# First attention of a macaron kernel: scores computed once and held in SBUF, the causal mask written by GpSimd

## What is computed

```python
scores = jnp.einsum('bqhd,bkhd->bhqk', qf, kf) * scale
mask = jnp.tril(jnp.ones((s, s), dtype=bool))
scores = jnp.where(mask[None, None], scores, jnp.finfo(scores.dtype).min)
p = jax.nn.softmax(scores, axis=-1)
o = jnp.einsum('bhqk,bkhd->bqhd', p, v).reshape(b, s, H * DV)
return o @ w_out
```

## Time and profile before

| what | value |
|---|---|
| median of 3 runs | 2211.37 us (2203.29 to 2222.01) |
| profiled execution | 2215.39 us |
| its span | 2213.7 us, 33049 instructions |
| PE busy | 1940.7 us (88%) |
| DVE busy | 1626.8 us (73%) |
| POOL busy | 991.4 us (45%) |
| ACT busy | 921.0 us (42%) |
| largest group | L1190 POOL, x528, 585.0 us |
| next | L1224 DVE x640, 385.6 us; L1231 DVE x640, 380.3 us; L1113 ACT x640, 358.0 us |

### The profile page before, as it was taken

One profiled execution on the slowest core, in us unless ns is written; L12 is line 12 of the kernel. 1 busy time (PEld: TensorE's weight loads), 2 busy tenths in 40 slices (PEclk: granted clock), 3 DMA queues, 4 the chain that ended last, 5 costly groups with the idle time before them and its releaser, 6 DMA issues. The chain is left out here.

```text
span 2213.7 us, 33049 instructions
## 1 busy us (share of the span) xinstructions
PE 1940.7 (88%) x10136; PEld 1107.0 (50%) x10136; DVE 1626.8 (73%) x2798; ACT 921.0 (42%) x1883; POOL 991.4 (45%) x892
## 2 busy tenths in 40 slices
PE   4756999999999999999999999977497899999996
PEld 3634555555555555555555555536364344444436
DVE  6766877877877877868868778747766887788726
ACT  1132444443343443343443443431123366777771
POOL 0014687586695685695695695630231100000010
PEclk8766999999999999999999999987697788999998
DMA  2200000000000000000000000010233020020001
GB/s 88 69 8 0 6 8 6 9 1 6 8 0 6 8 0 6 8 1 5 8 1 5 0 1 1 1 41 1 74 67 68 1 30 1 1 30 2 2 1 38
DMA packets 26709, 34.26 MB, mean 15 GB/s; under 512 B 5312, under 2 KB 19648, under 8 KB 26432
## 3 DMA queue, kind: packets, MB, share of 16 engines
q1 hardware_dynamic: 25360, 31.28, 5.9%
q10 hardware_dynamic: 1200, 1.31, 0.2%
HBM read 26.03 MB, written 6.29 MB: 15 GB/s over the span
## 5 line engine op out<-in xcount | busy, mean ns | idle before, releaser
L1113 ACT ACTIVATE lath_probs<-lath_shifted 128x512 f32<-128x512 f32 (+3 forms) x640 | 358.0, 565 | 685.6 <-DVE lath_shifted L1224 647.4
L1190 POOL TENSOR_TENSOR lath_summed<-lath_summed,lath_probs 128x512 f32<-128x512 f32 (+3 forms) x528 | 585.0, 1130 | 123.1 <-ACT lath_probs L1113 113.2
L1224 DVE TENSOR_TENSOR lath_shifted<-lath_score,lath_shift 128x512 f32<-128x512 f32 (+3 forms) x640 | 385.6, 607 | 149.2 <-PE lath_score L999 134.1
L1231 DVE TENSOR_REDUCE lath_maxima<-lath_max 128x1 f32<-128x512 f32 (+3 forms) x640 | 380.3, 605 | 132.8 <-PE lath_max L1020 85.8
L1878 ACT ACTIVATE atth_probs<-atth_score 128x512 f32<-128x512 f32 (+3 forms) x640 | 293.3, 541 | 165.8 <-PE atth_score L1797 163.6
L1837 DVE TENSOR_REDUCE atth_maxima<-atth_slot 128x2 f32<-128x1024 f32 (+3 forms) x288 | 286.2, 1042 | 61.4 <-PE atth_slot L1780 60.0
L1007 PE MATMUL lath_out<-lath_probs,lat_latent 128*64 128x512 f32 (+3 forms) x1280 | 308.9, 562 | 0.0
L1020 PE MATMUL lath_max<-lat_key_hi,lath_query_hi 128*128 128x512 f32 (+3 forms) x640 | 266.0, 424 | 17.4 <-DVE lath_maxima L1231 15.8
L995 PE MATMUL lath_score<-lath_query_hi,lat_key_hi 128*128 128x512 f32 (+3 forms) x640 | 266.7, 417 | 3.9 <-DVE lath_shifted L1224 3.9
L999 PE MATMUL lath_score<-lath_query_hi,lat_key_lo 128*128 128x512 f32 (+3 forms) x640 | 256.4, 401 | 0.0
L1725 POOL TENSOR_SCALAR_AFFINE_SELECT atth_probs<-atth_probs 128x512 f32<-128x512 f32 x64 | 40.8, 637 | 443.1 <-ACT atth_probs L1878 443.1
(11 more groups left out here) (342 smaller groups left out, 2794.9 us busy)
## 6 DMA issues: line engine op xcount, KB each, us to landing
att_first_query<-att_scratch SPq DMA_DIRECT2D x12, 256.0 KB, 8.9
atth_query<-att_scratch SPq DMA_DIRECT2D x12, 256.0 KB, 9.0
ffn_a_w<-in_L_ffn_W SPq DMA_DIRECT2D x2, 1024.0 KB
lat_raw_out<-in_L_attn_w_out SPq DMA_DIRECT2D x8, 256.0 KB, 2.7
lat_rope<-in_c_rope_feature SPq DMA_DIRECT2D x1, 2048.0 KB, 10.5
ffn_b_w<-in_L_ffn_W SPq DMA_DIRECT2D x2, 1024.0 KB, 7.1
mix_a_factors<-in_L_ffn_factors SPq DMA_DIRECT2D x8, 256.0 KB, 4.2
att_scratch<-attp_high SPq DMA_DIRECT2D x4, 512.0 KB, 3.3
```

Of the source, the lines that this page charges most:

```text
L1113: nc.scalar.activation(probs[:, prob_slot(j, kt), h, q0:CH], shifted[:, 2 * (kt % 2) + h, q0:CH], ACT.Exp, scale=SCALE0).then_inc(s["exp_d ...
L1190: last = nc.gpsimd.tensor_tensor(summed[:, j % 2, h, q0:CH], so_far, probs[:, prob_slot(j, kt), h, q0:CH], ALU.add)
L1224: nc.vector.tensor_tensor(shifted[:, 2 * (kt % 2) + h, q0:CH], score_bank[score_place(j, kt, h) % 3][:, q0:CH], shift[:, j % 2, h, q0:CH], ...
L1231: nc.vector.reduce_max(maxima[:, h, i, kc:kc + 1], max_bank[(i * (nj + 1) + kc) % 2][:, 0:width], AX.X).then_inc(s["maxima_taken"], 1)
```

## The change

The first pass goes. A unit of work is now one head, one chunk; a step is two key tiles of it, 1024 columns off the diagonal. PE makes the three products once, into a bank pair of 1024 columns; ACT copies them (L1077 of the changed kernel) into a ring of 14 steps in SBUF, `held`. On the diagonal POOL overwrites what lies ahead of the query with -1e30 in `held` (L1159, two selects of 128 columns a step). DVE takes the elementwise maximum of the held tiles into `largest` (L1200), PE turns the result by four transposes (L1002), and DVE reduces it to the row maxima (L1236); diagonal and spread follow as before. Then comes the second pass over the same slots: DVE adds `shift` in place (L1250), ACT takes the exponential in place (L1082), PE multiplies with the latent tile (L996, one key tile of the two in each half of the partitions, so that a `fold` on ACT and DVE adds the halves), and POOL sums (L1168, L1177). The sums of a unit are turned by four products with one column each.

The hand-written table is replaced by `latent_plan`, which lists every event with an engine, a cost, a rank and what it must follow, and orders each engine's list by simulating them with these costs. Nothing runs in a loop any more: all waits are against constants. Side work takes turns in two banks instead of having one, and `end_bank` is gone.

```diff
-LATENT_MAXIMA_STEPS = [(-12.0, -2.0), (0.2, 3.15), (3.5, 11.25), (12.2, 22.7)]
-LATENT_QUERY_STEPS = [(-21.0, -18.0), (-15.0, -13.0), (-5.8, -2.5), (8.5, 10.4)]
...
-LATENT_LAG = 2
-PROB_SLOTS = 5
...
+LATENT_UNITS = [(pair, j, h) for pair in range(PAIRS) for j in range(NCH) for h in range(2)]
+LATENT_STEPS = [(u, s) for u, (_, j, _) in enumerate(LATENT_UNITS) for s in range(key_tiles(j) // 2)]
+FIRST_STEP = [LATENT_STEPS.index((u, 0)) for u in range(len(LATENT_UNITS))] + [len(LATENT_STEPS)]
+PER_PAIR = 2 * NCH
+HELD_STEPS = 14
+SECOND_PASS_AFTER = 12.0
+QUERY_SLOTS = 3
...
+    for g, (u, s) in enumerate(LATENT_STEPS):
+        p, j, h = LATENT_UNITS[u]
+        widths = [(CH - q0) * (tiles.stop - tiles.start) for tiles, q0 in step_parts(g)]
+        total, late = sum(widths), g + SECOND_PASS_AFTER
+        elementwise = sum(0.07 + w / 960 for w in widths)
+        on_scalar = sum(0.1 + w / 1200 for w in widths)
+        held = g - HELD_STEPS
+        add("tensor", 0.1 + 3 * total / 2250, g, ("scores", g), ("low", u), of("scores", g - 1), of("evac", g - 2))
+        add("scalar", on_scalar, g, ("evac", g), ("scores", g), of("values", held), of("sum", held))
+        if s >= 2 * j:
+            add("pool", 0.6, g + 0.5, ("mask", g), ("evac", g))
+        add("vector", 0.0 if j and s == 0 else elementwise + (0.6 if j and s == 2 * j + 1 else 0.0), g + 1.0, ("max", g), ("mask", g) if s >= 2 * j else ("evac", g),
+            of("max", g - 1), of("turn_max", u - 2) if s == 0 else None)
+        add("vector", elementwise, late - 1.0, ("add", g), ("spread_out", u), ("max", g), of("add", g - 1))
+        add("scalar", on_scalar, late - 0.6, ("exp", g), ("add", g), of("exp", g - 1))
+        add("tensor", 0.12 + widths[0] / (1 if len(widths) > 1 else 2) / 540, late, ("values", g), ("exp", g), of("values", g - 1),
+            of("fold", u - 2) if s == 0 else None)
+        add("pool", sum_parts(g) * 0.06 + (CH if sum_parts(g) == 1 else total) / 420, late, ("sum", g), ("exp", g), of("sum", g - 1),
+            of("sums", u - 2) if s == 0 else None)
...
-        maxima = sb("maxima", [P, 2, TPC, NCH])
...
-        shifted = sb("shifted", [P, 4, CH])
-        probs = sb("probs", [P, PROB_SLOTS, 2, CH])
-        summed = sb("summed", [P, 2, 2, CH])
...
-        score_bank = [ctx.enter_context(nc.psum_tensor(f"lath_score{i}", [P, CH], F32)) for i in range(3)]
-        max_bank = [ctx.enter_context(nc.psum_tensor(f"lath_max{i}", [P, CH], F32)) for i in range(2)]
...
+        largest = sb("largest", [P, 2, 2, CH])
...
+        held = sb("held", [P, HELD_STEPS, 2, CH])
...
+        score_bank = [ctx.enter_context(nc.psum_tensor(f"lath_score{i}", [P, 2, CH], F32)) for i in range(2)]
+        out_bank = [ctx.enter_context(nc.psum_tensor(f"lath_out{i}", [P, CH], F32)) for i in range(2)]
+        side_bank = [ctx.enter_context(nc.psum_tensor(f"lath_side{i}", [P, CH], F32)) for i in range(2)]
...
-                                nc.tensor.matmul(bank[:, q0:q0 + P], core.ident_b, core.mask_kq, start=False, stop=False)
...
-                            mm = nc.tensor.matmul(bank[:, 0:width], query_hi[:, nj, h, i * P:(i + 1) * P],
-                                                  key_hi[:, kc * CH:kc * CH + width], start=True, stop=(kc < nj))
-                            if kc == nj:
-                                mm = nc.tensor.matmul(bank[:, width - P:width], core.ident_b, core.mask_qk, start=False, stop=True)
...
+                    elif kind == "turn_max":
+                        pe.wait_ge(s["maxed"], MAX_DONE[FIRST_STEP[n + 1] - 1])
+                        for i in range(TPC):
+                            last = nc.tensor.transpose(bank[:, i * P:(i + 1) * P], largest[:, n % 2, 0, i * P:(i + 1) * P], core.ident)
+                        last.then_inc(s["side_done"], 1)
...
-                            nc.scalar.activation(probs[:, prob_slot(j, kt), h, q0:CH], shifted[:, 2 * (kt % 2) + h, q0:CH], ACT.Exp,
-                                                 scale=SCALE0).then_inc(s["exp_done"], 1)
...
+                    if kind == "evac":
+                        act.wait_ge(s["scores_done"], n + 1)
+                        if n >= HELD_STEPS:
+                            act.wait_ge(s["values_done"], n - HELD_STEPS + 1)
+                            act.wait_ge(s["tiles_summed"], SUMS_DONE[n - HELD_STEPS])
+                        for tiles, q0 in step_parts(n):
+                            nc.scalar.activation(slot(n)[:, tiles, q0:CH], score_bank[n % 2][:, tiles, q0:CH], ACT.Copy)\
+                              .then_inc(s["evacuated"], 1)
+                    elif kind == "exp":
+                        for k, (tiles, q0) in enumerate(step_parts(n)):
+                            act.wait_ge(s["shift_added"], PARTS_DONE[n] - len(step_parts(n)) + k + 1)
+                            nc.scalar.activation(slot(n)[:, tiles, q0:CH], slot(n)[:, tiles, q0:CH], ACT.Exp, scale=SCALE0)\
+                              .then_inc(s["exp_done"], 1)
...
-                                last = nc.gpsimd.tensor_tensor(summed[:, j % 2, h, q0:CH], so_far, probs[:, prob_slot(j, kt), h, q0:CH], ALU.add)
...
+                    if kind == "mask":
+                        u, step = LATENT_STEPS[n]
+                        _, j, _ = LATENT_UNITS[u]
+                        pool.wait_ge(s["evacuated"], PARTS_DONE[n])
+                        for i in range(2):
+                            q0 = queries_from(2 * step + i, j)
+                            own = slot(n)[:, i, q0:q0 + P]
+                            nc.gpsimd.affine_select(own, own, [[1, P]], ALU.is_ge, MASKED, base=0, channel_multiplier=-1).then_inc(s["masked"], 1)
...
+                            nc.gpsimd.tensor_tensor(total[:, q0:CH], so_far, slot(n)[:, i, q0:CH], ALU.add).then_inc(s["tiles_summed"], 1)
...
-                            nc.vector.tensor_tensor(shifted[:, 2 * (kt % 2) + h, q0:CH], score_bank[score_place(j, kt, h) % 3][:, q0:CH],
-                                                    shift[:, j % 2, h, q0:CH], ALU.add).then_inc(s["shift_added"], 1)
...
-                            nc.vector.reduce_max(maxima[:, h, i, kc:kc + 1], max_bank[(i * (nj + 1) + kc) % 2][:, 0:width],
-                                                 AX.X).then_inc(s["maxima_taken"], 1)
...
+                def raise_largest(out, first, second, before):
+                    if before:
+                        dve.wait_ge(s["maxed"], before)
+                    nc.vector.tensor_tensor(out, first, second, ALU.max).then_inc(s["maxed"], 1)
...
+                    if kind == "max":
+                        u, step = LATENT_STEPS[n]
+                        _, j, _ = LATENT_UNITS[u]
+                        top, before = largest[:, u % 2], MAX_DONE[n] - max_parts(n)
+                        if step >= 2 * j:
+                            dve.wait_ge(s["masked"], 4 * u + 2 * (step - 2 * j) + 2)
+                        else:
+                            dve.wait_ge(s["evacuated"], PARTS_DONE[n])
+                        if step == 0 and u >= 2:
+                            wait_side(dve, ("turn_max", u - 2))
+                        if j == 0:
+                            for i in range(2):
+                                q0 = queries_from(2 * step + i, j)
+                                if step == 0 and i == 0:
+                                    nc.vector.tensor_copy(top[:, 0, :], slot(n)[:, 0, :]).then_inc(s["maxed"], 1)
+                                else:
+                                    raise_largest(top[:, 0, q0:CH], top[:, 0, q0:CH], slot(n)[:, i, q0:CH], before + i)
+                        elif step == 1:
+                            raise_largest(top, slot(n - 1), slot(n), 0)
+                        elif step:
+                            for tiles, q0 in step_parts(n):
+                                raise_largest(top[:, tiles, q0:CH], top[:, tiles, q0:CH], slot(n)[:, tiles, q0:CH], before)
+                            if step == 2 * j + 1:
+                                raise_largest(top[:, 0, :], top[:, 0, :], top[:, 1, :], MAX_DONE[n] - 1)
+                    elif kind == "turn_max_out":
...
+                    elif kind == "add":
+                        u, step = LATENT_STEPS[n]
+                        if step == 0:
+                            dve.wait_ge(freed(("spread", u)), use["spread", u] // 2 + 1)
+                        dve.wait_ge(s["maxed"], MAX_DONE[FIRST_STEP[u + 1] - 1])
+                        for tiles, q0 in step_parts(n):
+                            count = tiles.stop - tiles.start
+                            nc.vector.tensor_tensor(slot(n)[:, tiles, q0:CH], slot(n)[:, tiles, q0:CH],
+                                                    shift[:, u % 2, q0:CH].unsqueeze(1).broadcast_to([P, count, CH - q0]), ALU.add)\
+                              .then_inc(s["shift_added"], 1)
```

797 lines of the change are left out of this document (388 added, 409 removed).

## The result

The changed kernel takes 2506.3 us (median of 4 runs, 2501.61 to 2512.3), the kernel before 2214.47 us beside it (4 runs, 2203.29 to 2222.01): ratio 1.1324, 95% interval 1.1267 to 1.1381. The forecast was 2486 us with a range of 2390 to 2640, and slower with a chance of 92%.

The account below looks back on a forecast made before the run. The prediction took the old stage as bound by score-bank handoffs, the changed one by VectorE-GpSimd turns: 1495 us held + 68 stalls + 35 ends = 1598, 271 over 1327, giving 2486 us, range 2390 to 2640.

Parts of the forecast that it names:

- The mechanism: Latent attention: VectorE instructions with two SBUF operands and GpSimd's additions take turns; stage 271 us longer.
- The sum of held times: Latent attention: turn-taking time of VectorE, 678 us, plus GpSimd, 817 us, gives 1495 us, against 886 before.
- ends and stalls: Latent attention: 35 us at the stage's ends and 68 us when neither engine holds, middle of 0 to 136.
- The means: VectorE's 1024-column additions and maxima average 2.2 to 2.4 us; GpSimd's 512-column sums 1.8 us or more.
- The masks: GpSimd's 256 selects: 0.30 us each undisturbed, 77 us in all; counted as taking turns, held 38 us.
- VectorE alone: VectorE's work in latent attention without turns: 986 us, no saving against 1000, with 1.22 us per 1024-column addition.
- The 29 us: Cheaper VectorE access from SBUF than PSUM would return this over 448 additions; the forecast counted nothing.
- TensorE and ScalarE: Neither bounds latent attention: TensorE about 800 us at full clock, shown 60 to 90% busy; ScalarE under 900 us.
- A: Rival: VectorE and GpSimd run side by side in latent attention and the fullest bounds; 1995 us in all, 8%.
- B: Rival: TensorE's clock falls to half and TensorE sets latent attention's pace; 2591 us in all, 18%.
- C: Rival: waits chain from late sums through masks and maxima to shifts, 15% stalls; 2642 us in all, 10%.
- unrolled loops: Loops unrolled throughout: register arithmetic before waits disappears, but saves nothing while TensorE has room.

Follow-up runs that it names:

- before, operand in SBUF: Kernel before, with the 640 shift additions reading a constant SBUF tile instead of the PSUM score bank: 2380.14 us, ratio 1.0799.
- maxima from PSUM: Changed kernel with masks added by TensorE products and elementwise maxima reading the PSUM score bank instead of the held tile: 2311.23 us, ratio 1.0483.
- writes only: Changed kernel with GpSimd's 592 sums replaced by memsets of about equal length into a separate tile, same waits: 2127.4 us.
- sums by TensorE: Changed kernel with probability sums made by a ones column in TensorE's value products; GpSimd's sums and the fold gone: 2221.32 us, ratio 1.0049.
- all three: Changed kernel with masks and sums made by TensorE and maxima read from PSUM: 2171.38 us, ratio 0.9844.
- the fourth product: Changed kernel with a low-by-low product added to every score tile, 640 more TensorE products: 2510.48 us, ratio 1.1335.
- the planner's costs: Changed kernel with the planner's VectorE and GpSimd costs raised to durations with turns; only the order changes: 2498.79 us, ratio 1.1324.
- sums shared: Changed kernel with TensorE masks and maxima from PSUM; TensorE sums even units only, GpSimd sums odd ones: 2252.13 us, ratio 1.0193.
- masks by TensorE: Changed kernel with masks added by 256 TensorE products and GpSimd's 256 selects removed: 2530.98 us, ratio 1.1443.
- products and selects: Changed kernel with 256 TensorE mask products added and every GpSimd select kept: 2511.16 us, ratio 1.1352.

## Why the prediction was right, point by point

**The mechanism** was right: two engines that are shown nearly full and wait for turns, VectorE for 524 of its 1510 us (986 alone), GpSimd for 386 of 1366 (980 alone). It was shown from three sides: one operand moved into SBUF brings the loss into the old kernel, reading taken from GpSimd removes it, one operand moved back into PSUM returns 212 to 220 of 239 us.

**The sum of held times**, 1495 us, and 103 us of ends and stalls gave 1598, against 1623 measured; the 25 us, less 10 in what follows, are most of the 20 us between 2486 and 2506. Three price checks agree to some 10%: more masks 37 us for 38, maxima 212 to 220 for 239, a cycle of 2.23 us for 1.09 + 1.12. The table sets the sums beside what the traces show, in the terms of the table of the masks:

| kernel | held, as summed before | turn-taking instruction under way | none under way |
|---|---|---|---|
| before | 886 | 988 | 339 |
| before, operand in SBUF | 1192 | 1267 | 227 |
| changed | 1495 | 1540 | 83 |
| maxima from PSUM | 1218 | 1273 | 153 |
| writes only | 931 | 1021 | 228 |
| sums by TensorE | 931 | 1034 | 315 |
| all three | 654 | 720 | 573 |

The second figure is 45 to 103 us above the first everywhere, since it counts whole instructions with their ends. So the held times add up in every kernel, and what changes the meaning of the sum is the last column. In the changed kernel it is 83 us where I had put 103. That was partly luck: the 68 us of stalls in it were the middle of a range and had no cause behind them. In the old kernel with an operand in SBUF the held time rose by 448 x 0.56 + 64 x (0.43 + 0.30 + 0.15) = 307 us and the span by only 167, because the last column gave back 111.

**The means were mis-sized.** "2.2 to 2.4 us in the mean" for 1024 columns: 1.77 (L1250) and 1.62 to 1.69 (L1200) came, and 2.2 to 2.3 only in the stretches of wide steps. (1.77 - 1.20) / 1.12 is half of a turn each, not one. The sums came to 1.68 us, not 1.8 or more, and GpSimd to 84% of the stage, not over 90; VectorE's 93% was right. The step that failed is that each instruction meets another: in 1623 - 1366 = 257 us of the stage GpSimd had none under way, and VectorE's 64 turned maxima, folds and outputs meet it without a turn.

**The masks.** 0.30 us undisturbed was right (287 ns is the shortest). The guess that they take turns was right too: by the rule of the Trainium skill ("SBUF — State Buffer", Who interferes with whom), every reading GpSimd instruction contends with a VectorE instruction that has two SBUF inputs, and the trace now shows it: the 40 selects that meet no such instruction take 287 to 299 ns, the other 216 take 612 in the median and 1857 at worst. So their busy time is 148 us, not 77, and the price of more of them is the held 37. That the kernel would be as much faster without them, as I expected later, was false: the turns went and the time did not.

**VectorE alone, 986 us**: 1.22 us for 1024 columns was right (1203 ns shortest, 1208 to 1213 with a PSUM operand). The 29 us that the Trainium skill ("VectorE: DVE Perf Modes", The TRN2 errata) promised for operands from SBUF were counted as nothing, and these two numbers show nothing of them.

**TensorE and ScalarE** were no bound: TensorE 74% busy at 0.83, inside "60 to 90% at a clock clearly below 0.96", ScalarE 766 us, under 900. Instructions with a PSUM operand kept 0.68 us.

**The rivals**: A (side by side, 1995 us) fell with the first row; B by the fourth product; C by the planner's costs, by the masks taken from GpSimd's list, and by VectorE's 7% of idle time, under its mark of 10%. That unrolled loops gave nothing was not tried by itself.

**Where I was wrong in the experiments**: six expectations were too low. In four (writes only, sums by TensorE, all three, sums shared) I took away the terms of the bound and let what was left hide completely: the turns that VectorE still meets, TensorE's shown busy time above the sum of its products, the pace of the units that were left as they were. The last column of the table, 228 to 573 us where turns no longer fill the stage, had no term in them. In the other two (operand in SBUF, maxima from PSUM) the error was 40 to 50 us. The seventh, masks by TensorE, had the wrong sign. The last one, products and selects, had the right time with a reason that the trace does not bear out.

## What to carry to other kernels

Before an elementwise step is moved from PSUM into SBUF, look what GpSimd reads at that time: the place of one operand decided here whether two engines worked side by side, and moving it back was worth over 210 us. In a profile, this contention is no wait: look at the shortest and longest duration of one shape, and at start and end times that interlock. When work is removed from the bound, work out the second bound, and what neither engine fills, before you promise the difference; and do not average bounds over units that run one after another.

## What the runs showed of the hardware that was not expected

- 256 short selects of GpSimd cost 48 us of turns when added and give back 31 when taken away, yet the kernel gets 37 us slower by the first and no faster by the second.
- A memset of GpSimd with 1.33 us under way leaves VectorE alone (80 additions of 1024 columns beside memsets, none over 1226 ns); an addition of the same length does not (up to 2321 ns).
- Two value products of 512 columns take 1.08 us as two halves of 64 rows and 1.88 us as two groups of 65, one after the other.
- TensorE, given a third more score products in a stage that others bound, was granted more clock (0.875 for 0.846 over the span) and took no more time.
